# Slot rows turned by DMA transposes of 16-bit planes instead of by TensorE

## The reference

```
x1 = x + attn(layernorm(x))
xn = layernorm(x1)
chosen = argmax(xn @ gate_w.T)            # one of 8 experts for each row
out = x1 + xn + xn @ expert_w[chosen].T   # ffn(xn) = xn + expert_out
```

## Time and profile before

| | us |
|---|---|
| median of 3 runs | 1007.43 (1007.35 to 1007.58) |
| the profiled execution | 1007.09 |
| its span in the trace | 1005.3 |
| PE busy | 966.4 (96%) |
| DVE busy | 674.9 (67%) |
| ACT busy | 408.1 (41%) |
| POOL busy | 402.1 (40%) |

### The profile page before, as it was taken

The page is one execution under the profiler, slowest core; times in us unless marked ns, Lnnn a source line. Parts: engine busy times, 40 slices in busy tenths (PEclk is TensorE's granted clock), DMA queues, the critical chain, the costliest instruction groups (busy, mean ns, idle before and its releaser), DMA issues. The chain is left out here.

```text
span 1005.3 us, 16387 instructions
## 1 busy us (share of the span) xinstructions
PE 966.4 (96%) x5009; PEld 792.6 (79%) x5010; DVE 674.9 (67%) x1655; ACT 408.1 (41%) x704; POOL 402.1 (40%) x522
## 2 busy tenths in 40 slices
PE   7999999999999999999999999999857999999995
PEld 6788888888888888888888888888646888888884
DVE  6677777777777777777777687776985444444442
ACT  5333333333333333333333332332546666666662
POOL 1041616345261634626163362615273333333332
PEclk9999999999999999999999999999979999999998
DMA  9051022121302212130221203112265555555441
GB/s 322 12 178 43 22 105 79 48 86 42 126 32 95 83 44 88 40 126 33 95 84 43 97 31 126 41 44 85 84 220 178 159 160 166 168 159 161 138 149 55
DMA packets 47324, 101.70 MB, mean 101 GB/s; under 512 B 5781, under 2 KB 6549, under 8 KB 47264
## 3 DMA queue, kind: packets, MB, share of 16 engines
q1 hardware_dynamic: 33680, 61.93, 19.1%
q0 software_dynamic: 10800, 33.70, 8.7%
q10 hardware_dynamic: 2784, 5.31, 1.6%
HBM read 64.85 MB, written 37.90 MB: 102 GB/s over the span
## 5 line engine op out<-in xcount | busy, mean ns | idle before, releaser
L412 POOL TENSOR_TENSOR y_biased<-y_biased,gate 128x512 f32<-128x512 f32 x60 | 91.3, 1521 | 144.4 <-DVE y_biased L764 144.4
L481 POOL DMA_INDIRECT out<-gate,ids x71 | 69.9, 984 | 153.9 <-DVE gate L1029 115.2
L1355 PE MATMUL y<-expert_hi,x1T_hi 128*128 x284 | 119.3, 420 | 3.9 <-DVE x1T_lo L1023 3.9
L1029 DVE TENSOR_TENSOR gate<-y,x_rows 128x512 f32<-128x512 f32 x71 | 49.1, 691 | 108.2 <-PE y L1355 108.2
L1355 PE MATMUL y<-expert_hi,x1T_lo 128*128 x284 | 112.7, 397 | 0.0
L1355 PE MATMUL y<-expert_lo,x1T_hi 128*128 x284 | 112.3, 395 | 0.0
L1065 PE MATMUL gates<-GwT_hi,xT_hi 128*128 128x512 f32 x256 | 104.8, 409 | 0.0
L1065 PE MATMUL y<-DwT_hi,xT_hi 128*128 128x512 f32 x256 | 101.9, 398 | 0.5 <-DVE gateT L696 0.5
L1066 PE MATMUL gates<-GwT_lo,xT_hi 128*128 128x512 f32 x256 | 100.8, 394 | 0.0
L1067 PE MATMUL gates<-GwT_hi,xT_lo 128*128 128x512 f32 x256 | 100.3, 392 | 0.0
L1067 PE MATMUL y<-DwT_hi,xT_lo 128*128 128x512 f32 x256 | 100.3, 392 | 0.0
(11 more groups left out here) (246 smaller groups left out, 2372.8 us busy)
## 6 DMA issues: line engine op xcount, KB each, us to landing
x_rows<-routed_rows SPq DMA_DIRECT2D x71, 258.0 KB, 2.6
x_in<-L_attn_x SPq DMA_DIRECT2D x32, 512.0 KB, 4.4
x_rows<-L_attn_x SPq DMA_DIRECT2D x32, 512.0 KB, 4.4
raw_weights<-L_ffn_expert_w ACTq DMA_DIRECT2D x5, 1024.0 KB, 7.3
raw_weights<-L_ffn_expert_w SPq DMA_DIRECT2D x3, 1024.0 KB, 8.9
routed_rows<-padrow SPq DMA_DIRECT2D x9, 258.0 KB
out<-gate,ids POOLq DMA_INDIRECT x71, 2.8
raw_weights<-L_attn_D_w SPq DMA_DIRECT2D x1, 1024.0 KB, 8.1
```

The source lines that it names most:

```text
L412: nc.gpsimd.tensor_tensor(yb[:, i, :], yb[:, i, :], gate[:, i, :], ALU.mult).then_inc(S_["gated"], 1)
L481: nc.gpsimd.indirect_dma_start(out=out_rows, out_offset=bass.IndirectOffsetOnAxis(ap=ids[m][:, 0:1], axis=0), in_=res[m], in_offset=None, ...
L1029: nc.vector.tensor_tensor(res[m], Y[m % 2][:], rows[m][:, 0:D], ALU.add).then_inc(S_["slot_result"], 1)
L1355: ins = nc.tensor.matmul(Y[m % 2][:], x2T[a][:, k, m % 2 * P:(m % 2 + 1) * P], flat[w][:, bass.ds(first + k * D, D)], start=(k == 0 and a ...
```

## The change

- **Slots.** PE no longer turns the slot rows. After ACT's norm, DVE's `slot_split` copies the fp32 row into `halves`, in which the 512 low 16-bit halves stand first and then the 512 high ones. SP issues one `dma_start_transpose` of that 128x1024 tile of 16-bit words into `flipped` (`flip`). ACT's `slot_merge` copies the 1024 words back interleaved, so that `merged` is the turned fp32 tile in SBUF. `slot_hi` and `slot_lo` then read `merged` instead of a PSUM bank. `halves` and `flipped` have two buffers each, `rnorm` and `merged` have one.
- **Order.** DVE's slot s is now sum(s - 1), lo(s + 1), split(s + 3). ACT's is merge(s + 1), hi(s + 1), norm(s + 3). SP's is load(s + 4), flip(s). The row buffers are eight, the result and row number buffers stay at four (R).
- **Base.** ACT's base activation and the column GAIN go. POOL's `plus_identity` adds the identity to the diagonal blocks of each expert's raw weights (four 128x128 additions for each expert), and the sum takes the raw row x1. PE's turning of an expert now waits for that addition. For experts 0 to 2 it is done in blocks 4 to 6. For experts 3 to 7 it stands in POOL's order before the pieces n = 10, 14, 18, 22 and 26.
- **Start of the slots.** Slot 0 is no longer turned ahead of the last four pieces. The first flip also waits for the last scatter (`rows_sent[1]`).

The diff, cut to what the prediction speaks of:

```diff
-    M = 4
+    M, R = 8, 4
...
-        rows = [xrow[0][:, m, :] for m in range(M)]
-        rnorm = [yb[:, m, :] for m in range(M)]
-        res = [gate[:, m, :] for m in range(M)]
+        rows = [xrow[m // NT][:, m % NT, :] for m in range(M)]
+        res = [gate[:, r, :] for r in range(R)]
+        rnorm, merged = yb[:, 0, :], yb[:, NT - 1, :]
+        halves = [yb[:, 1 + q, :].bitcast(u16) for q in range(2)]
+        flipped = [raw[:, 2, q, :].bitcast(u16).rearrange("p (k t) -> p k t", t=P) for q in range(2)]
...
+            def flip(s, q):
+                counted_waits(sp, (S_["slot_halves"], s + 1), (S_["slot_merged"], s - 1))
+                sp.dma_start_transpose(flipped[q], halves[q]).then_inc(slot_flip[q], 16)
+            AHEAD = 4
+            for m in range(AHEAD):
                 load_slot(m, m)
             sp.wait_ge(S_["ends_ready"], 1)
             for e in range(E):
                 end = sp.value_load(end_rows[0:1, e:e + 1], min_val=0, max_val=DUMMY - P)
                 sp.dma_start(routed[bass.ds(end, P), :], padrow[:]).then_inc(S_["pad_sent"], 16)
+            sp.wait_ge(rows_sent[1], 16 * NT * (NBLK // 2))
+            for m in range(AHEAD, M):
+                load_slot(m, m)
+                flip(m - AHEAD, m % 2)
             with sp.Fori(1, EARLY) as u:
                 for m in range(M):
                     load_slot(u * M + m, m)
-            sp.wait_ge(rows_sent[1], 16 * NT * (NBLK // 2))
+                    flip(u * M + m - AHEAD, m % 2)
             sp.wait_ge(S_["pad_sent"], 16 * (E + 1))
             sp.wait_ge(S_["row_table"], 2)
             with sp.Fori(EARLY, FULL) as u:
                 for m in range(M):
                     load_slot(u * M + m, m)
+                    flip(u * M + m - AHEAD, m % 2)
             for s in range(FULL * M, SLOTS):
                 load_slot(s, s % M)
+                flip(s - AHEAD, s % 2)
+            for s in range(SLOTS - AHEAD, SLOTS):
+                flip(s, s % 2)
...
-                nc.gpsimd.tensor_scalar(xrow[q][:, :, GAIN], xrow[q][:, :, RSTD], 1.0, None, ALU.add
-                                        ).then_inc(S_["gain_ready"], 1)
...
+            def plus_identity(e):
+                pool.wait_ge(raw_loaded[e % RING], RAW_NEED[e % RING] + 16 * (e // RING + 1))
+                for f in range(KD):
+                    part = raw[:, e % RING, f, f * P:(f + 1) * P]
+                    nc.gpsimd.tensor_tensor(part, part, ident[:], ALU.add).then_inc(S_["expert_plus"], 1)
             rstd1(0)
             for b in range(NBLK):
                 body(b, b % 2)
+                if 4 <= b < 4 + RING:
+                    plus_identity(b - 4)
             def experts(first, end):
-                for n in filter(by_pool, range(first, end)):
+                for n in range(first, end):
+                    if n % KD == KD - 2 and RING <= n // KD + 1 < E:
+                        plus_identity(n // KD + 1)
+                    if not by_pool(n):
+                        continue
...
+                r, rturn = m % R, turn * (M // R) + m // R
+                counted_waits(pool, (row_loaded[m], 16 * (turn + 1)), (out_sent[r], 16 * rturn))
+                nc.gpsimd.tensor_copy(ids[r][:], rows[m].bitcast(i32)[:, TID:TID + 1]).then_inc(S_["slot_ids"], 1)
+            def slot_store(s, r):
                 counted_waits(pool, (S_["slot_result"], s + 1), (S_["slot_ids"], s + 1))
                 nc.gpsimd.indirect_dma_start(
-                    out=out_rows, out_offset=bass.IndirectOffsetOnAxis(ap=ids[m][:, 0:1], axis=0),
-                    in_=res[m], in_offset=None, bounds_check=OOB - 1, oob_is_err=False
-                ).then_inc(out_sent[m], 16)
+                    out=out_rows, out_offset=bass.IndirectOffsetOnAxis(ap=ids[r][:, 0:1], axis=0),
+                    in_=res[r], in_offset=None, bounds_check=OOB - 1, oob_is_err=False
+                ).then_inc(out_sent[r], 16)
...
+            def slot_merge(s, q, pair):
+                counted_waits(act, (slot_flip[q], 16 * (pair + 1)), (S_["slot_lo"], s))
+                nc.scalar.activation(merged.bitcast(u16).rearrange("p (t h) -> p h t", h=2),
+                                     flipped[q].rearrange("p (h k) t -> p h (k t)", h=2), ACT.Copy
+                                     ).then_inc(S_["slot_merged"], 1)
             def slot_hi(s, q):
-                act.wait_ge(S_["slot_turned"], s + 1)
+                act.wait_ge(S_["slot_merged"], s + 1)
                 wait(act, S_["slot_psum"], s - 1)
-                nc.scalar.activation(x2T[0][:, :, q * P:(q + 1) * P], by_block((TP, SC)[q]), ACT.Copy).then_inc(S_["slot_hi"], 1)
+                nc.scalar.activation(x2T[0][:, :, q * P:(q + 1) * P], by_block(merged), ACT.Copy).then_inc(S_["slot_hi"], 1)
             def slot_norm(s, m, turn):
                 act.wait_ge(row_loaded[m], 16 * (turn + 1))
-                wait(act, S_["slot_turned"], s - M + 1)
-                nc.scalar.activation(rnorm[m], rows[m][:, 0:D], ACT.Identity, bias=rows[m][:, SHIFT:SHIFT + 1],
+                wait(act, S_["slot_halves"], s)
+                nc.scalar.activation(rnorm, rows[m][:, 0:D], ACT.Identity, bias=rows[m][:, SHIFT:SHIFT + 1],
                                      scale=rows[m][:, RSTD:RSTD + 1]).then_inc(S_["slot_norm"], 1)
-            def slot_base(s, m):
-                nc.scalar.activation(rows[m][:, 0:D], rows[m][:, 0:D], ACT.Identity, bias=rows[m][:, SHIFT:SHIFT + 1],
-                                     scale=rows[m][:, GAIN:GAIN + 1]).then_inc(S_["slot_base"], 1)
             def slot(s, m, turn):
-                slot_hi(s, m % 2)
-                if not (isinstance(s, int) and s == SLOTS - 1):
-                    slot_norm(s + 1, (m + 1) % M, turn + (m + 1) // M)
-                    slot_base(s + 1, (m + 1) % M)
+                if not (isinstance(s, int) and s + 1 >= SLOTS):
+                    slot_merge(s + 1, (m + 1) % 2, turn * (M // 2) + (m + 1) // 2)
+                    slot_hi(s + 1, (m + 1) % 2)
+                if not (isinstance(s, int) and s + 3 >= SLOTS):
+                    slot_norm(s + 3, (m + 3) % M, turn + (m + 3) // M)
             slot_norm(0, 0, 0)
-            slot_base(0, 0)
-            slot(0, 0, 0)
             experts(E_STEPS[5], NE)
-            for s in range(1, M):
+            slot_norm(1, 1, 0)
+            slot_norm(2, 2, 0)
+            slot_merge(0, 0, 0)
+            slot_hi(0, 0)
+            for s in range(M):
...
+            def slot_split(s, q, pair):
+                dve.wait_ge(S_["slot_norm"], s + 1)
+                wait(dve, slot_flip[q], 16 * pair)
+                nc.vector.tensor_copy(halves[q].rearrange("p (h d) -> p h d", h=2),
+                                      rnorm.bitcast(u16).rearrange("p (d h) -> p h d", h=2)).then_inc(S_["slot_halves"], 1)
             def slot_lo(s, q):
                 dve.wait_ge(S_["slot_hi"], s + 1)
                 hi, lo = [h[:, :, q * P:(q + 1) * P] for h in x2T]
-                nc.vector.tensor_tensor(lo, by_block((TP, SC)[q]), hi.bitcast(f32), ALU.subtract).then_inc(S_["slot_lo"], 1)
+                nc.vector.tensor_tensor(lo, by_block(merged), hi.bitcast(f32), ALU.subtract).then_inc(S_["slot_lo"], 1)
             def slot_sum(s, m, turn):
+                r, rturn = m % R, turn * (M // R) + m // R
                 dve.wait_ge(S_["slot_psum"], s + 1)
-                dve.wait_ge(S_["slot_base"], s + 1)
-                wait(dve, out_sent[m], 16 * turn)
-                nc.vector.tensor_tensor(res[m], Y[m % 2][:], rows[m][:, 0:D], ALU.add).then_inc(S_["slot_result"], 1)
+                wait(dve, out_sent[r], 16 * rturn)
+                nc.vector.tensor_tensor(res[r], Y[m % 2][:], rows[m][:, 0:D], ALU.add).then_inc(S_["slot_result"], 1)
             def slot(s, m, turn):
-                slot_lo(s, m % 2)
+                last = s if isinstance(s, int) else 0
                 if not (isinstance(s, int) and s == 0):
                     slot_sum(s - 1, (m - 1) % M, turn - (m == 0))
+                if last + 1 < SLOTS:
+                    slot_lo(s + 1, (m + 1) % 2)
+                if last + 3 < SLOTS:
+                    slot_split(s + 3, (m + 3) % 2, turn * (M // 2) + (m + 3) // 2)
             experts(E_STEPS[2], E_STEPS[5])
-            slot(0, 0, 0)
+            slot_split(0, 0, 0)
             experts(E_STEPS[5], NE)
-            for s in range(1, 2 * M):
+            slot_split(1, 1, 0)
+            slot_split(2, 0, 1)
+            slot_lo(0, 0)
+            for s in range(M):
...
-                    pe.wait_ge(raw_loaded[e % RING], RAW_NEED[e % RING] + 16 * (e // RING + 1))
+                    pe.wait_ge(S_["expert_plus"], KD * (e + 1))
...
-            def slot_turn(s, m):
-                bank = (TP, SC)[m % 2]
-                pe.wait_ge(S_["slot_norm"], s + 1)
-                wait(pe, S_["slot_lo"], s - 1)
-                for k in range(KD):
```

(53 more changed lines are left out.)

3 lines of the change are left out of this document (removed).

## The result

The changed kernel takes 1045.49 us (median of 4 runs, 1045.15 to 1048.19), against 1007.5 for the kernel before: a ratio of 1.0381, 95% interval 1.0363 to 1.0399. The forecast was slower, 1030 us, with 992 to 1100 as the range. The direction was right and the size too small. The profiled execution has a span of 1043.4 us, 38.1 more than before.

The account below looks back on a forecast made before the run. PE was taken to bound the slots, but not the experts' stage. Span 1005.3 + 9.4 (longer slots) + 13 (later first product) = 1027.7, plus 1.8 around it 1029.5, with the profiled execution 0.3 below the median 1030 us; range 992 to 1100.

Parts of the forecast that it names:

- PE binds before: Slots: PE is the bound at 3.236 us a slot; removing its turns gains at most 30.5 us.
- The closed loop of two slots: Slots: split, flip, merge, high and low part (or norm) span two slots: 3.24 us plus the flip's landing time.
- F = 3.5 us: Slots: the flip's landing time, taken between two loads' times; makes a slot 3.37 us, 9.4 us more in all.
- The merge at 1.05 us: Slots: ACT's merge priced at 1.05 us, from the only 1024-element row.
- Rival 1: Slots: the flip is as cheap as a load, landing in 2.6 us; 998 us in all; chance 0.27.
- Rival 2: Slots: flips fill the DMA engines; 1046 us at 3.6 us a slot, 1116 at 4.6; chance 0.20.
- SP's own work: Slots: only the flip's landing was counted; the load queued behind was called harmless; issue might cost 32 cycles a tile.
- Rivals 3 and 4: Slots: transpose goes word by word, over 1500 us, chance 0.03; PE's clock sinks in the pauses, 1185 us, chance 0.05.
- my own case: Whole kernel: flip lands in 2.9 to 4.4 us, time 1009 to 1061 us; chance 0.45.
- The experts' stage, +13: Before the slots: POOL's additions and the later start move the first product from 764.47 to 777.7, +13 us.
- the best case that I had named: Experts' stage: is_top slips through at a POOL gap near 753, +3 us instead of +7.0.
- +16 with flip(0) late: Experts' stage: the first product comes 16 us later if the first flip is late.

Follow-up runs that it names:

- The deeper pipeline: Changed kernel with four buffers each for halves and flipped instead of two, norm and split four slots ahead instead of three: 1025.0 us (1.0174).
- the small loads: Changed kernel with the slots' row loads cut to the last four columns, 2 KB instead of 258 KB a slot: 1036.8 us (1.0283).
- the idle flips: Kernel before plus one DMA transpose of a fixed tile per slot, which only the next but one waits for: 1018.2 us (1.0112).

## Why the prediction was right, and where it was small

- **PE binds before** (30.5 us to gain at most): right. A quarter of the turning kept gave 20.5 us of the 23 asked.
- **The closed loop of two slots decides**: right, link by link, by the twin over norm. A round is 7.07 us in the chain. The deeper pipeline won 20 us without shortening any part of it.
- **F = 3.5 us**, chosen between 2.6 and 7.3: right in the middle of the slots (3.46), with up to 4.2 in the first ones. But I got to it by luck: I took the middle between two loads, as if it grew with its bytes, and most of it is fixed (2.8 us for half of them).
- **The merge at 1.05 us is the term that was too small.** It took 1.37. In the loop half of the difference counts, so by this sum it makes 70 x 0.16 = 11.3 us of the 14.4 by which the slots exceeded the forecast. The row that I took had 1024 fp32 elements in one piece. The merge reads and writes 16-bit words, the writes 4 bytes apart. Which of the two costs the 0.32 us was not tried. The remaining 3 us fit the slower flips of the first slots (163 matmuls from 800 to 850 us, 172 in each of the next two stretches).
- **Rival 1** (a flip like a load, 2.6 us; 998): wrong. The Trainium skill's sentence that transpose DMAs are as fast as regular ones (Advanced Engine Details and Errata, X-Bar Transpose (TRN2)) differs from the trace: 1.44 us of engine time for 256 KB, against 0.99 for a load of 258 KB, and 3.1 us to landing beside the small loads, against 2.6.
- **Rival 2** (full queues): wrong as the first bound, open as the second. I priced it at 2.6 us a slot for a flip at a load's price and 3.6 at twice. It is 3.2 in the changed kernel and 3.4 beside the idle flips.
- **SP's own work was put at nothing.** The prediction counts the flip's landing, and that a load queued behind it is harmless. SP's 3.09 us a slot do not bind at 3.58, so the forecast did not suffer. But the 2.80 us of PE that rival 1 hoped for were out of reach whatever F was. Even 3.14, as with the small loads, would win only 70 x 0.1 = 7 us in the slots, against 14 lost ahead of them (an estimate from these two numbers). The prediction also let SP's price grow with the flip's tiles; it took 1.25 us for a whole flip and 1.20 to 1.24 for half of one.
- **Rivals 3 and 4**: wrong. The clock stays at 1.00 from 800 to 950 us, in spite of PE's pause in each slot. In the first 21 us of the slots it is 0.92, and it was 0.95 in the first 36 before, so this costs no more than it did.
- **The range**: my own case stands once as 1009 to 1061 and once as 1012 to 1061. F = 2.9 gives 1009. Nothing hangs on it.
- **The experts' stage, +13**: 14.3, right in sum and partly by another way. Four additions take 1.68 us (I had 1.6). is_top did not wait until 757.0; POOL was idle from 752.42 to 753.28 and let it through at 753.19, the best case that I had named. But piece 20 stands ahead of the ranks in PE's order and waited for plus(5) until 757.47. So the later dest came at 758.7 all the same, and the last scatter was issued from 759.68 to 764.47, where I had 759.5 to 764.3. From there the chain of waits runs as I had it: plus(6), PE's turning at 766.22, ACT's copies, split(0), split(1), norm(2), merge, high and low part, with the first product 1.1 us after my 777.7. The landing of the last scatter, which I had only as "+16 with flip(0) late", is not on this chain. It binds once the additions are gone, and that is why removing them gave 7.85 us and not all of the 14.3.

The places where is_top got through and where the ranks waited, DVE in order of time:

```profile
753.19 0.19 DVE L826 TENSOR_TENSOR is_top<-score_sums,top_score 128x32 f32<-128x32 f32 x1
...
758.27 0.19 DVE L842 TENSOR_TENSOR list_position<-scores,list_ends 128x32 f32<-128x32 f32 x1 [2.46 <-PE scores L1226]
```

## What to carry to other kernels

Work taken off the bounding engine is only won if the new path closes in time: write down the loop that the buffers and the in-order queues form, add its durations, and divide by the slots that it spans. Then add up what the shared DMA engines are asked for in a slot (here a transpose DMA costs them 1.44 us, a plain load of the same size 0.99), and what the engine that issues the DMAs is asked for: its issues and register reads, here 3.1 us a slot where they had been 1.4. If these are tight, move half of the work: here every second slot gave 1.0% where all of them cost 3.8%, and it did so only after the flip stood ahead of a load that waits for something else.

## What the runs showed of the hardware

- A DMA transpose of 128x1024 16-bit words within SBUF takes 1.44 us of all 16 DMA engines (worked out with a load at 0.99; 1.57 in the run with idle flips), 1059 packets, 1.25 us of issue on SP, and 3.1 to 3.5 us to landing beside other traffic, 4.8 to 5.0 in the runs with a DMA share near 1. 128x512 words take 2.8 to 3.0 to landing, and 1.20 to 1.24 of issue.
- SP's register read from SBUF ahead of each load takes 0.27 us (median) without flips, 0.34 to 0.35 with a half flip ahead of it, and 0.61 to 0.75 with a whole one, at DMA shares from 0.65 to 1.01.
- ACT copies 1024 words of 16 bits in 1.37 us and 512 in 0.79, against 0.63 for 512 fp32 elements.
- A DVE copy from SBUF to SBUF can be held up beside POOL's tensor-tensor work, as is_top was before. In the run without the identity one split took 2.48 us instead of 0.70 and ended 0.56 us after a run of two POOL pieces that had started before it:

```profile
758.42 2.48 DVE L1058 COPY y_biased<-y_biased 128x1024 uint16<-128x1024 uint16 x1
```

```profile
757.84 2.50 POOL L491 TENSOR_TENSOR expert_lo<-expert_lo,expert_hi 128x512 fp32r<-128x512 f32 x2
```
